# Another order for the opening of an attention and mixture-of-experts kernel: values and averages, batches on TensorE, moments of the second chunk

## What is computed

```python
def attention(q, k, Wq, Wk, Wv, Wo):            # q = layernorm(x)
    sim = einsum('bqd,bkd->bqk', q @ Wq.T, k @ Wk.T)
    mean = jnp.mean(sim, axis=(1, 2), keepdims=True)
    var = jnp.var(sim, axis=(1, 2), keepdims=True)
    attn = softmax((sim - mean) * rsqrt(var + EPS), axis=-1)
    return einsum('bqk,bkd->bqd', attn, k @ Wv.T) @ Wo.T
x = x + attention(layernorm(x), ctx_768, Wq, Wk, Wv, Wo)
h = layernorm(x)
probs = softmax(h @ gate_w + gate_b); cw = probs kept where they are among the two best
x = x + swiglu(h @ sw1 + sb1) @ sw2 + sb2 + sum_e cw[e] * (swiglu(h @ rw1[e] + rb1[e]) @ rw2[e] + rb2[e])
```

## Time and profile before

| | |
|---|---|
| time, median of 3 runs | 145.19 us (145.05 to 146.31) |
| profiled execution, its own time | 145.23 us |
| its span in the trace | 143.1 us |
| mean granted clock of PE | 0.988 |
| PE busy | 129.5 us, 90% |
| PEld busy | 93.5 us, 65% |
| DVE busy | 103.1 us, 72% |
| ACT busy | 70.6 us, 49% |
| POOL busy | 23.7 us, 17% |

### The profile page before, as it was taken

How to read it: one execution, slowest core, us unless ns; L and a number is a source line. 1 busy time by engine, 2 the same in 40 slices (tenths; PEclk the granted TensorE clock), 3 DMA queues, 4 the chain that set the end, 5 groups by cost and what they waited for, 6 DMA issues and landing times.

```text
span 143.1 us, 1983 instructions
## 1 busy us (share of the span) xinstructions
PE 129.5 (90%) x597; PEld 93.5 (65%) x597; DVE 103.1 (72%) x305; ACT 70.6 (49%) x133; POOL 23.7 (17%) x41
## 2 busy tenths in 40 slices
PE   0997888799989997999999997999899899999981
PEld 0785676688757665687877674787576557766641
DVE  1676885699979988829949985649969683855642
ACT  2447955993330359933640379923221964213230
POOL 7083414049300010500300010002100000000000
PEclk9999999869999999999999999999999999999999
DMA  4999100001810000078020000086010008820002
GB/s 129 288 351 262 49 2 5 0 2 53 341 50 0 5 0 2 5 249 338 0 73 5 0 0 0 15 301 282 27 46 0 0 5 251 336 73 7 0 0 73
DMA packets 8796, 12.96 MB, mean 91 GB/s; under 512 B 1305, under 2 KB 6962, under 8 KB 8274
## 3 DMA queue, kind: packets, MB, share of 16 engines
q1 hardware_dynamic: 8210, 12.61, 25.5%
q10 hardware_dynamic: 576, 0.23, 0.6%
HBM read 11.72 MB, written 1.11 MB: 90 GB/s over the span
## 4 chain that ended last, share of the span: by engine, by line
issue 43%; PE 35%; POOL 7%; ACT 6%; DVE 4%; DMA 2%; POOLq 1%; DVEq 0%; ACTq 0%
PE bank L844 31%; POOL row_powers L358 3%; DMA ctx_sb<-in_ctx_dram 2%; POOL w_rest L380 2%; POOL ln_rstd L367 2%; ACT prob L448 2%; PE bank L860 1%; POOLq L51 1%; POOL sim_r L373 1%; PE bank L852 1%; ACT L470 1%; ACT v_sb L438 1%; DVE xn L615 1%; PE bank L928 1%; PE bank L1001 1%
## 5 line engine op out<-in xcount | busy, mean ns | idle before, releaser
L497 ACT ACTIVATE silu<-bank,b_cols 128x512 f32<-128x512 f32 (+1 forms) x37 | 24.9, 675 | 44.7 <-PE bank L844 44.3
L844 PE MATMUL bank<-x_head,w_head 128*128 128x512 f32 x72 | 39.3, 545 | 0.0
L844 PE MATMUL bank<-act,w_sb 128*128 128x512 f32 (+1 forms) x74 | 36.4, 580 | 0.0
L750 DVE TENSOR_TENSOR silu<-silu,cw_all 128x512 f32<-128x512 f32 (+1 forms) x31 | 20.8, 671 | 15.4 <-DMA cw_all<-cw_dram 7.8
L844 PE MATMUL bank<-x_rest,w_head 128*128 128x512 f32 x72 | 28.6, 398 | 0.0
L758 DVE SCALAR_TENSOR_TENSOR act<-bank,b_cols,silu 128x512 f32<-128x512 f32 (+1 forms) x37 | 27.2, 736 | 1.9 <-ACT silu L497 1.0
L844 PE MATMUL bank<-x_head,w_rest 128*128 128x512 f32 x72 | 28.6, 397 | 0.0
L844 PEld LDWEIGHTS bank<-x_head,w_head 128*128 128x128 f32 x72 | 13.6, 189 | 7.5 <-issue 4.6
L844 PEld LDWEIGHTS bank<-x_rest,w_head 128*128 128x128 f32 x72 | 13.6, 189 | 6.7 <-issue 5.3
L844 PEld LDWEIGHTS bank<-act,w_sb 128*128 128x128 f32 x74 | 13.7, 188 | 3.8 <-issue 1.0
L844 PEld LDWEIGHTS bank<-x_head,w_rest 128*128 128x128 f32 x72 | 13.7, 190 | 3.4
(11 more groups left out here) (110 smaller groups left out, 171.5 us busy)
## 6 DMA issues: line engine op xcount, KB each, us to landing
cw_all<-cw_dram SPq DMA_DIRECT2D x4, 1024.0 KB, 7.0
cw_all<-cw_dram SPq DMA_DIRECT2D x4, 512.0 KB, 5.0
cw_all<-cw_dram SPq DMA_DIRECT2D x6, 256.0 KB, 3.7
x_sb<-in_x_dram SPq DMA_DIRECT2D x4, 256.0 KB, 4.5
w_sb<-in_L_ffn_rw_dram SPq DMA_DIRECT2D x1, 1024.0 KB, 7.5
ctx_sb<-in_ctx_dram SPq DMA_DIRECT2D x4, 192.0 KB, 4.6
out_dram<-x SPq DMA_DIRECT2D x3, 256.0 KB, 2.1
w_sb<-in_L_ffn_rw_dram SPq DMA_DIRECT2D x1, 512.0 KB, 7.0
```

Source lines behind the costliest of these rows:

```text
L497: scalar.activation(silu[:, k, cols], HID[(2 * n) % 3][:, cols], ACT.Silu, bias=b1_cols[:, 0, e:e + 1]).then_inc(silu_sb, 1)
L750: dve.tensor_tensor(silu[:, k, cols], silu[:, k, cols], cw_all[:, e - 1, cols], ALU.mult).then_inc(scaled_sb, 1)
L844: return pe.matmul(dst, lhs, rhs, start=start, stop=stop, skip_group_check=True)
```

## The change

PE: `scores`, `transpose_prob`, `attend` and `transpose_x2` are divided into functions for one batch. In the opening `transpose_x(1)` moves from ahead of `project_v(0)` and `scores_average(0)` to behind `project_u(1)`; the two batches of scores(1), the transposes of chunk 0's exponentials and the two halves of attend(0) are interleaved; `transpose_x(2)` fills the place ahead of the second attend; `transpose_ctx(2)` and `project_u(2)` move up, `scores_average(1)` moves down behind `project_v(2)`, and `transpose_x2` of the two batches stands in two places.

ACT: casts 0 and 1 move up ahead of the copy of vo_w; x_copy(1) moves behind u_copy(1); prob_copy(0) stands between the third and the fourth exponential; x_copy(2) and ctx_copy(2) move up; cast 2 moves behind x_copy(2), cast 3 behind ctx_copy(2), cast 4 behind v_copy(2), just ahead of chunk 1's exponentials.

DVE: the second maximum of chunk 0 moves behind the variance; chunk 1's moments move behind the first group's normalised tiles, and its second maximum behind the second group's; scores_scale(1) moves behind both x2_rests.

```diff
@@ scalar
+            scalar.wait_ge(gate_in, 16)
+            split_heads(0, 1)
+            scalar.wait_ge(sw1_in, 16)
+            split_heads(1, 2)
             scalar.wait_ge(setup_ps, 2)
             copy(vo_w[:, :], bank[0][0:DC, D:2 * D]).then_inc(setup_sb, 1)
             ctx_copy(1)
-            x_copy(1)
             v_copy(0)
             u_copy(1)
-            scalar.wait_ge(gate_in, 16)
-            split_heads(0, 1)
-            scalar.wait_ge(sw1_in, 16)
-            split_heads(1, 2)
-            scalar.wait_ge(rw1_in, 16)
-            split_heads(2, 3)
-            exponentials(0)
-            prob_copy(0)
-            prob_copy(1)
-            split_heads(3, 5)
+            x_copy(1)
+            scalar.wait_ge(negmax_sb, 1)
+            exponential(0, 0, 0)
+            exponential(0, 0, 1).then_inc(prob_sb, 1)
+            exponential(0, 1, 0)
+            prob_copy(0)
+            exponential(0, 1, 1).then_inc(prob_sb, 1)
+            prob_copy(1)
+            x_copy(2)
+            scalar.wait_ge(rw1_in, 16)
+            split_heads(2, 3)
+            ctx_copy(2)
+            split_heads(3, 4)
             v_copy(1)
...
-            ctx_copy(2)
-            x_copy(2)
             u_copy(2)
             x2_heads(0, 0)
+            x2_heads(0, 1)
             v_copy(2)
-            x2_heads(0, 1)
+            split_heads(4, 5)
             exponentials(1)
@@ vector
-            for c in range(2):
-                scores_statistics(CB * c)
-                scores_statistics(CB * c + 1)
-                scores_moments(c)
-                scores_maxima(CB * c)
-                scores_maxima(CB * c + 1)
-                if c == 0:
-                    scores_variance(0)
-                    scores_scale(0)
+            scores_statistics(0)
+            scores_statistics(1)
+            scores_moments(0)
+            scores_maxima(0)
+            scores_variance(0)
+            scores_maxima(1)
+            scores_scale(0)
+            scores_statistics(2)
+            scores_maxima(2)
+            scores_statistics(3)
             for g in range(CB):
                 residual(0, g)
                 second_statistics(0, g)
             second_normalise(0, 0)
+            scores_moments(1)
+            second_normalise(0, 1)
+            scores_maxima(3)
             scores_variance(1)
-            second_normalise(0, 1)
             x2_rests(0, 0)
+            x2_rests(0, 1)
             scores_scale(1)
-            x2_rests(0, 1)
@@ tensor
             transpose_ctx(1)
-            transpose_x(1)
             pe.wait_ge(setup_sb, 2)
             project_v(0)
             scores_average(0)
             project_u(1)
-            scores(1)
-            transpose_prob(0)
-            attend(0)
+            transpose_x(1)
+            pe.wait_ge(xt_sb, 2)
+            batch_scores(1, 0)
+            transpose_batch_prob(0, 0)
+            batch_scores(1, 1)
+            pe.wait_ge(v_ready, 1)
+            attend_group(0, 0)
+            transpose_batch_prob(0, 1)
+            transpose_x(2)
+            attend_group(0, 1)
+            transpose_ctx(2)
             project_v(1)
...
+            project_u(2)
+            transpose_x2(0, 0)
+            project_v(2)
             scores_average(1)
-            transpose_ctx(2)
-            transpose_x(2)
-            project_u(2)
-            project_v(2)
-            transpose_x2(0)
+            transpose_x2(0, 1)
             router(0)
```

More of the change, by code:

```diff
@@ L438, in v_copy, with exponential @@
                 copy(v_sb[:, c].rearrange("p t d -> p (t d)"), values(c)[:, :]).then_inc(v_ready, 1)
+            def exponential(c, j, i):
+                return scalar.activation(prob[:, j, i, :], early(c)[j][:, i * S:(i + 1) * S], ACT.Exp,
+                                         bias=neg_max[:, IB * j + i:IB * j + i + 1],
+                                         scale=row_scale[:, IB * j + i:IB * j + i + 1],
+                                         accum_out=row_sum[:, j, i:i + 1])
             def exponentials(c):
@@ L447, in exponentials @@
                     for i in range(IB):
[L448 to L451, removed]
+                        last = exponential(c, j, i)
                     last.then_inc(prob_sb, 1)
@@ L526, in _ @@
             split_heads(1, 2)
+            scalar.wait_ge(setup_ps, 2)
+            copy(vo_w[:, :], bank[0][0:DC, D:2 * D]).then_inc(setup_sb, 1)
+            ctx_copy(1)
+            v_copy(0)
+            u_copy(1)
+            x_copy(1)
[7 more added lines that the diff above has]
+            x_copy(2)
             scalar.wait_ge(rw1_in, 16)
             split_heads(2, 3)
-            exponentials(0)
-            prob_copy(0)
-            prob_copy(1)
-            split_heads(3, 5)
+            ctx_copy(2)
+            split_heads(3, 4)
             v_copy(1)
@@ L875, in project_v, with batch_scores @@
                 last.then_inc(v_ps, 1)
+            def batch_scores(c, j):
+                pe.wait_ge(u_ready, upto_batch(c, j) if c == 0 and j == 0 else done(c))
+                for i in range(IB):
+                    q = (IB * j + i) * P
+                    last = mm(early(c)[j][:, i * S:(i + 1) * S], x_t[:, c % 2, q:q + P], u_sb[:, c % 2, j * S:(j + 1) * S])
+                last.then_inc(sim_ps, 1)
             def scores(c):
@@ L882, in scores @@
                 for j in range(CB):
[L883 to L887, removed]
+                    batch_scores(c, j)
             def scores_average(c):
@@ L897, in scores_average, with transpose_batch_prob @@
                 mm(average(c)[:, 0:4 * TC], mean_of_partitions[:, :], sim_mom[:, :, :, :].rearrange("p k t h -> p (k t h)")).then_inc(simavg_ps, 1)
+            def transpose_batch_prob(c, j):
+                pe.wait_ge(prob_sb, CB * c + j + 1)
+                for k in range(IB):
+                    for i in range(IB):
+                        last = pe.transpose(PROB[j][:, k * S + i * P:k * S + (i + 1) * P],
+                                            prob[:, j, i, k * P:(k + 1) * P], ident[:, :])
+                last.then_inc(probt_ps, 1)
@@ L899, in transpose_prob @@
             def transpose_prob(c):
                 for j in range(CB):
[L901 to L906, removed]
+                    transpose_batch_prob(c, j)
@@ L908, in attend, with attend_group @@
+            def attend_group(c, g):
+                for j in groups(c)[g]:
+                    pe.wait_ge(probt_sb, CB * c + j + 1)
+                    for i in range(IB):
+                        for k in range(IB):
+                            last = mm(late(c, g)[:, (IB * j + i) * D:(IB * j + i + 1) * D], prob_t[:, j, k, i * P:(i + 1) * P],
+                                      v_sb[:, c, IB * j + k, :], start=k == 0, stop=k == IB - 1)
+                last.then_inc(attn_ps, 1)
             def attend(c):
@@ L909, in attend @@
                 pe.wait_ge(v_ready, c + 1)
[L910 to L920, removed]
@@ L923, in transpose_x2 @@
[L923 to L929, removed]
+                pe.wait_ge(cwt_sb, c)
+                pe.wait_ge(cwrow_sb, c)
+                attend_group(c, 0)
@@ L931, in router, with transpose_x2 @@
+            def transpose_x2(c, g):
+                pe.wait_ge(xn_ready, upto(c, g))
+                pe.wait_ge(x1_ready, upto(c, g))
+                for i in batch_tiles(groups(c)[g]):
+                    last = pe.transpose(late(c, g)[:, i * P:(i + 1) * P], xn[:, i, :], ident[:, :])
+                last.then_inc(x2t_ps, 1)
             def router(c):
@@ L1046, in _ @@
                       "scores_average": scores_average, "transpose_prob": transpose_prob, "attend": attend,
-                      "transpose_x2": transpose_x2, "router": router, "transpose_cw": transpose_cw}
+                      "transpose_x2": lambda c: transpose_x2(c, 0), "router": router, "transpose_cw": transpose_cw}
             def run(n, place):
```

5 lines of the change are left out of this document (removed).

## The result

| | before | changed |
|---|---|---|
| median of 22 runs | 145.42 us (144.91 to 146.50) | 144.63 us (144.21 to 146.36) |
| profiled execution, its own time | 145.23 us | 144.33 us |
| span | 143.1 us | 142.2 us |

The ratio of the two is 0.9942, with a 95% interval of 0.9921 to 0.9963: the change takes off 0.58%, or 0.84 us (0.54 to 1.15 by the interval). The forecast was a gain of 0.86, and 144.3 us counted from the 145.19 of three runs; by 22 runs the kernel before takes 145.42.

The account below looks back on a forecast made before the run. The prediction took PE to bound the loop, so only an earlier opening counts, through two chains to DVE's product at 34.01. The 0.86 us gained there, off the 145.19 median, gave 144.3 us, range 143.4 to 145.4.

Parts of the forecast that it names:

- What bounds: Whole kernel: steady loop bound by PE; opening's last wait is PE's 0.59 us at 40.70, for DVE's tiles of chunk 1.
- First average and exponentials: Chunk 0 in the opening: variance and sim_r 0.60 us earlier, first exponential at 13.5 instead of 14.27, gaining 0.75.
- Batch by batch: Chunk 0's attention: first batch gains 0.8 us, second ends at 19.7 instead of 19.20; DVE waits 0.3 for it.
- The cast of 128x512: ACT's cast at 19.0, POOL's subtraction at 19.7 delaying both ln_rstd; first normalised tiles at 21.7 against 21.90.
- The second scale: Chunk 1's scale on DVE: exponentials of chunk 1 start at 25.65 instead of 25.77, so only 0.12 us comes through.
- Behind it: After chunk 1's exponentials: DVE's product at 33.15 instead of 34.01, gain 0.86 us; PE's wait shrinks to about 0.25.
- The number: Whole kernel time: 145.19 us less the 0.86 gained on DVE, giving 144.3 us.
- The rule that speaks against it: DVE and POOL lock a shared port; no stall taken for DVE's first normalised tiles beside POOL's second ln_rstd at 21.65.
- The later exponentials (1): Opening: ln_rstd, late cast or longer subtraction delays chunk 1's exponentials to 26.35; gain 0.1, time 145.1 us; chance 0.22.
- The faster chain (2): Opening from 17.4 on: chunk 1's exponentials near 25.1, together 1.5 us gained, time 143.7 us; chance 0.22.
- The clock (3): Half-clock stretch near 29 to 30 moves behind 32.4, costing 1.7 us, time 146.0 us; chance 0.10.

Follow-up runs that it names:

- e1: Kernel before, with DVE's statistics of x(2) moved ahead of x2_rests(0, 0), so ln_veps is not beside POOL's subtractions; ratio to before 0.9952.
- e6: Changed kernel, with one wait on POOL holding its small subtractions until chunk 0's negative maxima are done; ratio to before 0.9886, median 144.20 us.
- e7: Changed kernel, POOL's small subtractions and that of 128x512 held behind chunk 0's and 1's negative maxima, ACT's cast 4 earlier; ratio to before 0.9868, median 144.03 us.
- e5: Changed kernel, with chunk 0's second maximum on DVE put back ahead of the variance; ratio to before 0.9976.
- e3: Changed kernel, with POOL's subtractions of the gate and of 128x256 moved ahead of scores_rstd(0); ratio to before 0.9926, six runs.
- e4: Changed kernel, POOL's small subtractions ahead of scores_rstd(0), that of 128x512 behind scores_rstd(1), ACT's cast 4 between the x2_heads; ratio to before 1.0005, median 145.79.
- e2: Changed kernel, with DVE's statistics of x(2) moved behind scores_scale(1), so no ln_veps is beside POOL's large subtractions; ratio to before 0.9950.

## Why the prediction was right, point by point

- **What bounds.** Right for the opening: the chain read back from PE's wait at 40.70 was the one to read, e1 took the stall away and PE's wait went with it. Not whole for the loop, which has the wait of 0.60 at 101.93 that a load sets.
- **First average and exponentials.** The average and variance came as summed (sim_r at 12.31; 12.4 was forecast), but the first exponential came at 13.92 instead of 13.5. This step failed: it kept neg_max at 0.17 while POOL's subtraction of 128x256, waiting for nothing since its cast had moved up, moved in beside it. The term that was missing is 0.47 on neg_max, and e6 shows it: without the overlap the distance is 3.63 instead of 3.99. Only 0.36 come through, because ACT's copy of x(1) then ends last.
- **Batch by batch.** Right in kind: the second attention starts at 18.84 (forecast 18.65), and DVE's wait for it is there, 0.58 instead of 0.3. The first exponential was 0.42 late and the second attention 0.19, so the steps between were summed 0.2 too long.
- **The cast of 128x512.** Right: POOL's subtraction at 19.87 (19.7), both ln_rstd right behind it (21.10, forecast 20.95), first tiles at 21.83 (21.7). e7 against e6 puts the price of this and of the last cast at 0.12.
- **The second scale.** Exponentials of chunk 1 at 25.77 instead of 25.65: nothing came through instead of 0.12; by the distances they are 0.08 later than before. Had no subtraction stood beside neg_max, they would have been 0.34 nearer to the copy, by e6, and so ahead of the forecast: the missed 0.47 hid behind steps that were summed too long.
- **Behind it.** Right in its mechanism, and this carried the result: the product started at 33.17 (33.15), the tiles at 39.88 (39.85), and the silu ended at 33.14 (33.1), the gap that ACT had waited for PE's transposes of the weights, 0.16, having closed. But DVE's selection of the experts took 1.3 behind the router's exponential, not 1.05, so cw_cols were ready at about 29.5 (29.2) and POOL's pair ended at 33.18 (32.9), with the silu and not before it. attend(1) came at 32.61 (32.4), waiting for cw_rows, and PE was through with its own work at 39.84 instead of 39.6, so that its wait went whole instead of leaving 0.25.
- **The number.** That 0.84 and 0.86 agree so closely is in part luck. The interval is 0.6 us wide, and by the distances, which leave out that this trace's copy of vo_w was 0.08 earlier, product and tiles gained 0.76 and 0.74. The forecast was 0.1 too high.
- **The rule that speaks against it.** I weighed it at the wrong place. At the first tiles it did not bite: 0.60 for two beside ln_rstd, as before. It bit at neg_max, beside a subtraction that I had taken from the list without asking what runs beside it. The Trainium skill (SBUF — State Buffer, section on SBUF's two separate sides) has a DVE operation with two inputs in SBUF blocked by a GpSimd operation that reads SBUF and came first. Four traces agree with it where POOL subtracts weights: neg_max 0.64 (changed kernel), 0.65 (e5), sim_mom 0.70 (e3), row_scale 1.23 (e4). The short power operations of POOL do not show it.
- **The rivals.** The later exponentials (1) did not come to pass in the changed kernel, but e4 is that rival made real: an operation of POOL that holds back a DVE operation of the chain, 1.13 us for the exponentials. The faster chain (2) was there to be had (e6, e7), not in this order. The clock (3): in the changed kernel's trace the granted clock is full throughout. The low stretch is in the traces of before, e1 and e7. In the changed order it costs nothing there (e7), in the old order it goes with the 0.3 us between the exponentials and attend(1), which DVE's stall covers in the kernel before. These traces have a mean clock of 0.988. The four executions of e1 with that mean are the fastest of its twelve (144.36 to 144.80), but the three of the changed kernel with a mean of at most 0.988 are among its slowest (145.41, 145.62, 146.36, with a median of all of 144.63). Where their low stretch lay and whether they started late is not on record, so what the clock costs there stays open.

## What to carry to other kernels

When an engine's filler work (here casts and subtractions of weights) is moved or loses its wait, look for what runs beside it as well as what waits behind it: on POOL and DVE a tiny operation on a critical chain can take as long as the large one beside it. A single wait that holds filler work back until the critical operation is done (e6) brought the traces 0.35 us, and moving it into an idle slot of POOL without that (e3, e4) lost 0.2 and 1.1. And before crediting a new order with its gain, try the one stall that it happens to dissolve: e1, with one moved piece, had two thirds of the shift at the tiles.

## What the runs showed of the hardware

- DVE operations of 128x4 or 128x8 with both inputs in SBUF took 0.16 to 0.17 us alone, and 0.64 to 1.23 us when POOL's subtraction of weights had started just before, ending within 0.05 us of it (e3: 11.70 against 11.68; e4: 26.85 against 26.83). ln_veps, 128x4 with one tensor as input, was held in the same way: 0.17 alone (e1), 1.78 beside the pair of 128x768 (before).
- DVE operations that take one input from PSUM, and the statistics, were not held: in the changed kernel the two residuals of the second batch ran from 20.10, in the middle of POOL's subtraction of 128x512 (19.87 to 21.14), and took 0.61 together, as the first batch's did at 17.84 with POOL idle:

```profile
17.84 0.61 DVE L686 SCALAR_TENSOR_TENSOR x<-bank,row_inv,x_sb 128x128 f32<-128x128 f32 x2 [0.28 <-PE bank L855]
...
20.10 0.61 DVE L686 SCALAR_TENSOR_TENSOR x<-bank,row_inv,x_sb 128x128 f32<-128x128 f32 x2 [0.58 <-PE bank L855]
```

- POOL's power operations (0.69 to 0.73 us on 128x2) held nothing in these traces: two tiles took 0.60 together right beside them, and sim_avg_sq, with both inputs in SBUF, its usual 0.16 at 22.62 beside ln_rstd of 22.07 to 22.80 (before).
- These executions differ by up to 1.3 us in the first 11 us, by when PE goes over to full pace, which is more than the whole change; distances from a mark behind the start told kernels apart to 0.03 us (e2 and the changed kernel agree at all five marks), where medians of 6 to 12 runs told them apart to some 0.4 to 0.6.
